# GpSimd makes both the high and the low part of x for the projections, one unit ahead

## The reference, cut to what matters

```
xn  = layernorm of x over j (per channel and row)
x1  = (xn - mean) * rsqrt(var + eps) * ln_w + ln_b      mean, var over everything
q, k, v, g = wq x1, wk x1, wv x1, sigmoid(wg x1 + bg)   128 outputs = 4 heads x 32, per (i, j)
scores[h,i,j,k] = sum_c q[h,c,i,j] k[h,c,i,k] / sqrt(32) + bias[h,i,j]
a   = softmax over k;   o = g * (a v);   x = x + wrep o + b      attention along each row i
t   = tokens of x (one per channel and row: 8192 tokens of 128)
t   = t + MoE(layernorm(t))     8 experts, top 2, 128 -> 512 -> 128, gelu
```

## Time and profile before

| | |
|---|---|
| median of three runs | 915.98 us |
| the profiled execution | 914.75 us, of which the span from first to last instruction is 913.0 us |
| PE busy | 697.1 us (76%) |
| DVE busy | 662.6 us (73%) |
| ACT busy | 618.9 us (68%) |
| POOL busy | 458.7 us (50%) |
| mean granted clock of PE | 0.898 of full speed |

### The profile page before, as it was taken

One profiled execution on the slowest core, in us unless ns is written; L12 is line 12 of the kernel. 1 busy time (PEld: TensorE's weight loads), 2 busy tenths in 40 slices (PEclk: granted clock), 3 DMA queues, 4 the chain that ended last, 5 costly groups with the idle time before them and its releaser, 6 DMA issues.

```text
span 913.0 us, 23230 instructions
## 1 busy us (share of the span) xinstructions
PE 697.1 (76%) x7225; PEld 566.8 (62%) x7226; DVE 662.6 (73%) x2359; ACT 618.9 (68%) x1548; POOL 458.7 (50%) x534
## 2 busy tenths in 40 slices
PE   0098988887996889679978636299888988999960
PEld 0097777775775667457756425278766767888850
DVE  3873788887777767876787584778766666899954
ACT  0954899996986669467866652078676767888850
POOL 4000333335533367357764771047777777566660
PEclk9999999998998879877988755599999999999995
DMA  9958400000000000000000132123232323554559
GB/s 216 271 139 169 39 2 2 2 2 1 2 2 2 1 16 31 4 7 25 31 22 20 39 92 56 39 54 84 83 87 81 87 82 93 144 130 115 144 144 242
DMA packets 66148, 63.99 MB, mean 70 GB/s; under 512 B 21381, under 2 KB 57286, under 8 KB 64520
## 3 DMA queue, kind: packets, MB, share of 16 engines
q1 hardware_dynamic: 55288, 37.65, 18.0%
q0 software_dynamic: 9152, 18.76, 6.3%
q10 hardware_dynamic: 1616, 6.42, 2.8%
HBM read 35.88 MB, written 26.93 MB: 69 GB/s over the span
## 4 chain that ended last, share of the span: by engine, by line
PE 50%; DVE 21%; POOL 10%; DMA 8%; issue 7%; SPq 2%; ACT 2%; POOLq 0%; ACTq 0%; DVEq 0%
PE PT L1494 7%; PE S L1320 4%; PE PT L1332 4%; POOL expert_out L726 4%; PE B L1362 4%; DMA shared<-in_L_conv_ln_b 4%; PE B L1275 3%; PE S L1477 3%; POOL routed L698 3%; DVE pl L971 3%; PE S L1479 2%; PE S L1478 2%; PE A L1287 2%; DVE on L997 2%; PE B L1347 2%
## 5 line engine op out<-in xcount | busy, mean ns | idle before, releaser
L726 POOL DMA_INDIRECT expert_out<-yo,rows_all x156 | 156.2, 1002 | 89.7 <-ACT yo L893 53.9
L885 ACT ACTIVATE hf<-S,b_sb,inv_hscale 128x256 f32<-128x256 f32 x312 | 150.6, 563 | 48.4 <-PE S L1479 48.0
L698 POOL DMA_INDIRECT routed<-pay,pos x128 | 124.7, 975 | 69.6 <-issue 34.5
L799 ACT ACTIVATE L<-L,lmin 128x128 f32<-128x128 f32 x512 | 159.2, 391 | 0.4
L682 POOL TENSOR_TENSOR og<-gt,on 128x256 f32<-128x256 f32 x64 | 46.5, 727 | 170.4 <-DVE on L997 170.0
L984 DVE CUSTOM_DVE_ANT_0 L<-S,biasN 128x128 f32<-128x128 f32 x512 | 117.3, 285 | 18.3 <-issue 16.8
L1228 DVE SCALAR_TENSOR_TENSOR hl<-hf,hscale,hh 128x512 f16<-128x512 f32 x156 | 117.5, 753 | 5.5
L1226 DVE TENSOR_SCALAR hh<-hf,hscale 128x512 f16<-128x512 f32 x156 | 77.0, 493 | 55.3 <-ACT hf L885 55.2
L794 ACT ACTIVATE ph<-PT 128x512 f16<-128x512 f32 x128 | 75.9, 595 | 29.4 <-PE B L1349 20.7
L1477 PE MATMUL S<-fx_h,w_h 128*128 128x256 f16 x312 | 86.3, 277 | 12.0 <-issue 10.8
L1332 PE MATMUL PT<-identity,L 128*128 128x128 f32 x512 | 84.7, 305 | 6.8 <-ACT L L799 4.5
(11 more groups left out here) (239 smaller groups left out, 1801.9 us busy)
## 6 DMA issues: line engine op xcount, KB each, us to landing
rows_all<-routed SPq DMA_DIRECT2D x78, 130.0 KB
shared<-expert_out SPq DMA_DIRECT2D x12, 384.0 KB, 6.5
shared<-in_L_ffn_W SPq DMA_DIRECT2D x8, 512.0 KB, 7.3
routed<-blank SPq DMA_DIRECT2D x30, 129.0 KB, 3.0
shared<-expert_out SPq DMA_DIRECT2D x16, 224.0 KB, 5.6
expert_out<-yo,rows_all POOLq DMA_INDIRECT x156
out<-xt SPq DMA_DIRECT2D x6, 384.0 KB
xt<-in_x SPq DMA_DIRECT2D x4, 512.0 KB, 13.4
```

The costliest lines, as they stand in the source:

```text
L698: pool.indirect_dma_start(routed[TABLE_OF[b]], bass.IndirectOffsetOnAxis(ap=pos[k][:, row:row + 1], axis=0), source[:, part_row(b, i), :], ...
L726: pool.indirect_dma_start(expert_out, bass.IndirectOffsetOnAxis(ap=row_place[t % IN_BUFS][:, k, W + 1:W + 2], axis=0), yo[t % YO_BUFS][:, ...
L799: last = nc.scalar.activation(L[p][:, h, i, :], L[p][:, h, i, :], ACT.Exp, scale=-1.0, bias=lmin[p][:, h * R + i:h * R + i + 1])
L885: last = nc.scalar.activation(hf[p][:, b, :], S[2 * p + pair][:, k * TILE:(k + 1) * TILE], ACT.Gelu, scale=inv_hscale[:, 0:1], bias=b1_fla ...
```

## The change

`high_x` leaves ACT, and `low_x` on POOL becomes `split_x`, which makes the high part by a copy (`tensor_copy` to F32R) and then the low part by the same subtract as before. In step s POOL now splits unit s+1, where it made the low part of unit s before; unit 0 is split ahead of the loop. `split_x` waits for x1 itself (x1_ready), for PE's use of the tile two units before (vg_full) and for its own gate. The wait for landed scatters moves from odd to even steps.

```
-            def low_x(u, p):
+            def split_x(u, p):
                 hi = slice(p * C, (p + 1) * C)
                 lo = slice((1 - p) * C, (2 - p) * C)
+                if u == 0:
+                    pool.wait_ge(x1_ready, 1)
+                if u == UNITS // CH:
+                    pool.wait_ge(x1_ready, 2 * CH)
+                wait(pool, vg_full, 2 * (u - 1))
+                wait(pool, og_ready, 2 * (u - 3))
+                high, low = (xs[p][k].rearrange("p (r w) -> p r w", w=W) for k in (hi, lo))
+                nc.gpsimd.tensor_copy(high, x1[hi, rows(u, p), :]).then_inc(xs_high, 1)
                 pool.wait_ge(xs_high, u + 1)
-                wait(pool, og_ready, 2 * (u - 2))
-                nc.gpsimd.tensor_tensor(xs[p][lo]..., x1[hi, rows(u, p), :], xs[p][hi]..., ALU.subtract).then_inc(xs_ready, 1)
+                nc.gpsimd.tensor_tensor(low, x1[hi, rows(u, p), :], high, ALU.subtract).then_inc(xs_ready, 1)
...
-                    pool.wait_ge(xs_ready, min(u + 3, UNITS) if isinstance(u, int) else u + 3)
+                    pool.wait_ge(xs_ready, min(u + 4, UNITS))
...
-                if p == 1 and s < UNITS:
+                if p == 0 and s + 1 < UNITS:
                     (wait until the earlier scatters have landed)
-                unit(s, p, 0, low_x)
+                unit(s + 1, 1 - p, 0, split_x)
                 if s in rows_at:
-                    pool.wait_ge(xs_ready, min(s + 1, UNITS))
+                    pool.wait_ge(xs_ready, min(s + 2, UNITS))
                     normal_rows(rows_at[s])
-                if p == 1 and s < UNITS and scatters_at[s]:
-                    pool.wait_ge(xs_ready, s + 1)
+                if p == 0 and s + 1 < UNITS and scatters_at[s]:
+                    pool.wait_ge(xs_ready, s + 2)
...
+            split_x(0, 0)
             attention_steps(step)
...
-            act.wait_ge(x1_ready, 1)
-            nc.scalar.activation(xs[0][0:C]..., x1[0:C, 0:R, :], ACT.Copy).then_inc(xs_high, 1)
...
-            def high_x(u, p):
-                wait(act, vg_full, 2 * (u - 1))
-                hi = slice(p * C, (p + 1) * C)
-                nc.scalar.activation(xs[p][hi]..., x1[hi, rows(u, p), :], ACT.Copy).then_inc(xs_high, 1)
...
                 unit(s, p, 2, high_p, 0)
-                if s:
-                    unit(s, p, 0, high_x)
                 unit(s, p, 2, high_p, 1)
```

More of the change, by code:

```diff
@@ L663, in _ @@
             last.then_inc(const_ready, 1)
-            def low_x(u, p):
+            def split_x(u, p):
                 hi = slice(p * C, (p + 1) * C)
                 lo = slice((1 - p) * C, (2 - p) * C)
+                if u == 0:
[6 more added lines that the diff above has]
+                nc.gpsimd.tensor_copy(high, x1[hi, rows(u, p), :]).then_inc(xs_high, 1)
                 pool.wait_ge(xs_high, u + 1)
-                wait(pool, og_ready, 2 * (u - 2))
-                nc.gpsimd.tensor_tensor(xs[p][lo].rearrange("p (r w) -> p r w", w=W), x1[hi, rows(u, p), :],
-                                        xs[p][hi].rearrange("p (r w) -> p r w", w=W), ALU.subtract).then_inc(xs_ready, 1)
+                nc.gpsimd.tensor_tensor(low, x1[hi, rows(u, p), :], high, ALU.subtract).then_inc(xs_ready, 1)
             def gate(u, p, half):
@@ L752, in _ @@
                 last.then_inc(rows_normal, 1)
-            act.wait_ge(x1_ready, 1)
-            nc.scalar.activation(xs[0][0:C].rearrange("p (r w) -> p r w", w=W), x1[0:C, 0:R, :], ACT.Copy).then_inc(xs_high, 1)
             for c in range(CH):
@@ L770, in _ @@
             nc.scalar.activation(qk[1][0], A[:], ACT.Copy).then_inc(qk_ready, 1)
-            def high_x(u, p):
-                wait(act, vg_full, 2 * (u - 1))
-                hi = slice(p * C, (p + 1) * C)
-                nc.scalar.activation(xs[p][hi].rearrange("p (r w) -> p r w", w=W), x1[hi, rows(u, p), :], ACT.Copy).then_inc(xs_high, 1)
             def copy_qk(u, p, n):
```

## The result

The changed kernel takes 919.5 us (median of 20 runs, 916.7 to 924.0); the kernel before, run beside it, 916.1 (20 runs). The ratio is 1.0036, 95% interval 1.0024 to 1.0049: 3.3 us longer, 2.2 to 4.5. That is no change by the prediction's own bound of 0.5%, and the time lies 0.1 us from the forecast.

A forecast was written before the change was run, and what follows sets the result against it. No engine full; a quiet step is a chain of waits through PE, DVE and POOL, without ACT. Collisions 2.8 + POOL-bound step 0.7 + scatter steps 0.1 + start 0 = 3.6 us, giving 919.6 (917 to 922); range 911.5 to 927.

The forecast's parts named there:

- The copy, 0.62 us: New 64x512 copy on POOL, once per unit: 0.62 us, from the small cast's 0.29 plus 0.33 by the fill's slope.
- rival 1: The POOL copy costs as much as the subtract, 1.27 us: 14 us slower in all, 930; chance 0.13.
- ACT's relief, 0: Removing ACT's copy (31 x 627 ns) gains 0, since nothing that ends a step waits for it; at most 8.2 us.
- rival 4: ACT's relief counts: 0.3 to 0.4 us won in some 23 steps, 8 less the 3.6: 911.6; chance 0.09.
- Moved ahead, 0: Splitting xs a whole step earlier on POOL: worth 0, since no PE instruction waited for xs.
- Row scales, 3 x 0.25: DVE's three row scales, held by POOL's copy and subtract: middle of +0.51 and nothing, 0.8 us together.
- Picks, 4 x 0.45 = 1.8: DVE's four top-2 picks: copy and subtract delay L1083 and L1085, +0.47 at one, about 0.45 each, 1.8 us.
- Casts, 0.2: DVE's three integer casts in the positions: the next two-input operation waits 0.08 us longer each, 0.2 together.
- The POOL-bound step, 0.7: Step from 418.9 where POOL runs without a gap and ACT's tanh waits for the gate: +0.70 us in full.
- Scatter steps, 0.1, and the start, 0: Five-scatter steps without normalising: slack leaves 0.1 us; start, units 0 and 1 split while DVE makes x1: 0, little spare.
- Rival 3: The copy does not hold DVE up; only the subtract does, 0.70 later: 1.2 us faster, 915; chance 0.24.
- Rival 2: PE's granted clock stays at 1.2 GHz longer after DVE stalls: 5 us more, 925, or the reverse, 914; 0.08 each way.

The follow-up runs named there:

- split behind the rows: Changed kernel with POOL's copy and subtract issued after the normalised rows and, in those steps, after DVE has made the scales: 911.4 us, ratio 0.9951.
- copy out at the nine: Changed kernel without POOL's copy in units 13, 19 to 21, 24 to 26, 30 and 31 (high part stale): 914.9 us, ratio 0.9992.

## Why the prediction was right, and where it was not

- *The copy, 0.62 us.* 0.61. Extending a small cast by the slope of the fill was right, and rival 1 falls.
- *ACT's relief, 0.* Right: quiet steps unchanged, and taking the copy out of ACT won nothing (rival 4 falls).
- *Moved ahead, 0.* The number was right for the move alone and wrong as a reading. No wait for xs said nothing on how near xs came: 0.3 us. The experiment with the copy added alone priced this at 12.4 us without the move. Its cover in quiet steps, which I ascribed to POOL's idle time, exists only because the unit is ahead.
- *Row scales, 3 x 0.25.* 0.27, 0.28 and 0.31. That is more right than its argument: I took the mean of "+0.51" and "nothing is lost, one-input operations follow". The second branch came, L502 slipped in first, and the one-input L503 was held for 1.14 us all the same. The prediction's own rows had such a case: the cast of 0.83 us at 402.66 has one input too.
- *Picks, 4 x 0.45 = 1.8.* The step that was mis-sized: 0.07, 0.03, 0.12, 0.30, together 0.5. The subtract fell on one operation at the end of the pick instead of one in its middle, and the copy fell on short operations with one end in it.
- *Casts, 0.2.* 0.1 for the positions as a whole, but as +0.68, +0.11 and -0.67; the gain in the last step was not foreseen.
- *The POOL-bound step, 0.7.* 0.87 (14.90 against 14.03). The price of what comes behind it was missed: +2.9 in step 28.
- *Scatter steps, 0.1, and the start, 0.* Steps 22 and 23 take 12.17 and 12.18 us as before, and PE's bias rows again 20.62 us. The first projection starts at 67.33, later than the 66.7 that was to be a sign of being wrong. It is not one: the transfer that the first piece of x1 waits for ended at 45.32 instead of 44.67, and counted from there PE starts alike. By the same count the last piece of x1 ends 1.7 us later, where I had said 2.8.
- *Rival 3, the copy does not hold DVE up.* It falls, by L501. The Trainium skill, "SBUF — State Buffer", section "Who interferes with whom", said so for DVE's two-input operations; the trace agrees with it here (0.49 us against 0.19 in the kernel with the split behind the rows), though not at POOL's normalising operations at 386.
- *Rival 2, the clock.* I gave it a chance of 0.08 each way and kept it apart from the sum. The direct terms come to 2.4 us (0.9 + 0.5 + 0.1 + 0.9), where I had 3.6. In the two pairs of traces the steps grow by 6.3; I ascribe the other 3.9 to the place of PE's low clock, of which steps 27 and 28 show 2.9, and the rest is only argued. In the medians, 3.3 (2.2 to 4.5) less 2.4 leaves 1 us, which the noise does not tell from nothing. The forecast hit in part by luck: direct terms 1.2 too high stand where the runs have about 1 us that no term of mine explains.

How far do the direct terms go over the other kernels? (The copy added alone is left out, as its quiet steps grow too.) The table has DVE's time for the three row scales, the four picks and the three positions, POOL's step 27, their sum, and the measured difference to the kernel before, by the ratio (us, each rounded by itself; means of two traces for before and after).
```
kernel                              DVE    step 27   sum    measured
before                              37.5    14.0     51.5     0
after                               39.0    14.9     53.9    +3.3
copy out at unit 27                 39.0    14.4     53.4    +3.5
copy out altogether                 37.0    14.1     51.2    -1.3
copy out at the nine                36.4    14.7     51.2    -0.7
copy twice                          36.6    15.6     52.2    +2.9
ACT's copy taken out                37.6    14.1     51.6    +3.0
one unit ahead, copy left to ACT    31.8    15.5     47.2    -2.0
split behind the rows               32.7    14.7     47.4    -4.5
the same, copy left to ACT          28.1    14.0     42.1   -11.4
```
Between after and the kernel without the copy the sum falls by 2.7 of the measured 4.6, and the large gains of the last rows go with it. It misses by 2 to 3 us in four rows: the copy twice, ACT's copy taken out and the one unit ahead are slower than it says, and they have steps 27 and 28 at 32.2, 30.0 and 32.3 us instead of 27.2; the fastest kernel is 2 us faster than it says. That fits a share of PE's clock, without showing it.

What stays open is why the clock falls inside step 27 in the kernel before and behind it in all others, and so whether the next edit will find such a place, and how much of the medians is the clock's at all.

## What to carry to other kernels

"Nothing waits for this buffer" is not "there is room": read the distance between the last write and the first read before anything is added in front. When a stage is made a step earlier, use the freedom to place it, since here the same instructions behind the normalised rows were 7.8 us better than ahead of them. And where an engine's clock falls after a stall, add up direct costs for the sign, but keep a range as wide as the clock's steps (2 to 4 us each here). A dose is a fair check only if the second helping falls on the same neighbours as the first: here it pushed the subtract off the picks, and the timeline had to be read again before the time said anything.

## What the hardware showed that I had not expected

- A copy on POOL with one input (64x512, 0.61 us) holds a two-input DVE operation to its end: L501 takes 0.49 us and ends 0.04 after it. POOL's normalising operations in the earlier trace rows did not hold the 96 columns of L1083 (0.28 us); its 128 columns took 0.42 us beside them at 291.17, and 0.29 in the kernel with one unit ahead, where POOL was idle. The subtract also holds a DVE operation with one SBUF input: L503 1.14 us instead of 0.17, L1112 1.28 instead of 0.17.
- A low clock costs nothing on a stretch that another engine bounds: 4.2 us of it in step 27 of the kernel before, with PE idle for 0.46 us instead of more than 3.
- Two PE stalls of the same 2.1 us in the same place of the program ended at 1.2 GHz in one kernel and at 2.4 in the other, 2.25 us apart in the step's length.
